# Next batch's rows turned in every attention unit, its first two Q slices in the last unit, and one PSUM bank each for V and K

## The chip, the cores and the metric

The kernel runs on one core of a Trainium2 chip. The metric is the device time of one execution in microseconds (us). TensorE (PE in the profile) multiplies and transposes, VectorE (DVE), ScalarE (ACT) and GpSimd (POOL) do the elementwise work, and SyncE (SP) issues most transfers.

## What is computed

A pre-norm transformer layer on four batches of 1024 tokens with 1024 channels: block-local attention with 16 heads, a set of 64 global query tokens per head that replace their rows of the result, and a linear layer.

```python
        q = _split_heads(hidden_states @ Wq + bq)
        k = _split_heads(hidden_states @ Wk + bk)
        v = _split_heads(hidden_states @ Wv + bv)
        ctx = _local_attention(q, k, v)      # query block of 128, keys from 64 before it to 64 behind it
        idx = _global_index(q)               # token 0, the 62 of largest norm, the last token, per head
        qg = jnp.take_along_axis(q, idx[..., None], axis=-2)
        g_scores = jnp.einsum('nhqd,nhkd->nhqk', qg, k) / math.sqrt(d)
        g_probs = jax.nn.softmax(g_scores, axis=-1)
        g_ctx = jnp.einsum('nhqk,nhkd->nhqd', g_probs, v)
        ctx = ctx.at[bn, bh, idx].set(g_ctx)
...
        w = weight * scale_weight[:, None]
        out = jnp.einsum('bsi,oi->bso', x, w) + bias
...
    x = L0_attn_hidden_states                # 4 batches, 1024 tokens, 1024 channels, 16 heads
    x = x + _L0_attn_ref(_layernorm(x, axis=-1), L0_attn_Wq, L0_attn_bq, L0_attn_Wk, L0_attn_bk, L0_attn_Wv, L0_attn_bv)
    x = x + _L0_ffn_ref(_layernorm(x, axis=-1), L0_ffn_weight, L0_ffn_scale_weight, L0_ffn_bias)
```

## The kernel before

Everything is float32 with split operands: each matmul operand x is held as x_hi (rounded) and x_lo (the rest), and a product is three matmuls, hi\*hi, lo\*hi and hi\*lo. A projection slice is 128 output channels (a pair of heads). One **half** of a slice (512 of the 1024 tokens) is 24 matmuls of 128x512 into one of the two PSUM banks of `proj`; a **part** is 12 of these 24.

For each batch n the program runs two phases.

- **The Q phase**: slices 0 to 7 of Q. PE projects a half, ACT takes it out of PSUM with the bias (`q_out`), PE turns it back to token rows (`turn_q`), ACT copies (`q_nat_out`) and SP stores it, and DVE takes the norms (`norm_of`). From slice 4 on DVE also runs the search for the largest norms of the first eight heads (`top_find`, 24 steps, then `top_rows`). PE turns norms into rows twice per batch (`turn_norms`). At the end of the phase V and K of pair 0 are projected.
- **Eight units**, one per pair of heads (`attend`, hp = 0 to 7; they are called unit 0 to unit 7 here). A unit has four steps of local attention (`scores`, `maxima`, `exps`, `turn_p`, `p_hi_out`, `p_lo_out`, `weigh`) and one global step. Between them, at eight fixed places, PE does part(0) to part(7). In units 0 to 6 these are the projections of V and K for the next unit. In unit 7 they are the transposes of the eight row tiles of the next batch (or, after the last batch, of the linear layer's weight), 8 transposes each, into the banks of `proj`; ACT then writes xT_hi and DVE xT_lo from there.

Each engine's order is written out by hand; nothing is scheduled. DVE's order at the end of a unit is `global_maxima`, `row_moments`, `pv_sums(3)`, `split_q` (two passes over 1024 columns), `k_lo_out(0)`, `gp_lo_out`, the layer norm's roots, `row_normalise`, `k_lo_out(1)`, `g_out`. In unit 3 the last steps of the second norm search and `top_rows` stand ahead of `split_q`. `k_lo_out` reads a half of K from its bank and is what frees it (`proj_free`); for V it is `v_out` on ACT.

In the code before, a half belongs to a bank: half 0 of V and of K goes to bank 0, half 1 of both to bank 1. In units 0 to 6 the parts are V half 0, V half 1, K half 0, K half 1, two parts each:

```python
b = k // 4
project_half(n, PAIRS + 2 + 2 * hp + b, b, n * BUFS + PAIRS // 2 + 1 + hp, (k // 2) % 2, (k % 2,))
```

`misc` is one more PSUM bank, in which the pieces of V (`turn_v`, three groups), the padded global query (`turn_gq`) and a small part of the global probabilities are turned, one after the other. `v_lo_out(2)` on DVE is the last reader of the third V group. POOL splits weights (`split`: a cast and a subtraction per slice, 1.1 and 2.5 us on average by the page) and scales the step results (`normalise`). SP is in order as well: rows, weights, stores.

## Time and profile before

| | |
|---|---|
| time, median of 3 runs | 2275.86 us (2275.55 to 2278.52) |
| span of the profiled execution | 2275.5 us |
| PE busy | 2192.1 us, 96% |
| weight loads, DVE, ACT, POOL busy | 82%, 68%, 37%, 26% |
| granted TensorE clock, mean | 0.991 |
| chain that ended last | PE 79%, DVE 15%, issue 4%, ACT 2% |

The chain that ended last is the way back from the last instruction to what released it. A timeline row says when a group of equal instructions began (us from the start of the span), how long it took, engine, line, what it writes and reads, how many, and in brackets how long the engine was idle before and what ended that. A window row gives the length of a stretch, each engine's busy time in it with its count, and then the granted clock.

### The profile page before, as it was taken

What the parts mean: (1) busy time and instruction counts of PE and PEld (TensorE: products, weight loads), DVE (VectorE), ACT (ScalarE), POOL (GpSimd) and SP (SyncE); (2) the same over time, 40 slices, a digit from 0 to 9 for tenths busy, and PEclk for the clock granted to TensorE, in tenths of its full rate; (3) what the DMA queues carried; (4) which work ended last, traced back from release to release, by engine and by line L of the source; (5) the groups of instructions that cost most, each with busy time, mean ns of one, the idle gap of its engine ahead of it and who ended that gap; (6) DMA issues with size and microseconds to landing.
All of it is one profiled execution on the core that took longest, in us unless ns stands there. A gap on an engine that the chain in (4) does not pass through costs nothing.

```text
span 2275.5 us, 41042 instructions
## 1 busy us (share of the span) xinstructions
PE 2192.1 (96%) x13024; PEld 1863.5 (82%) x13024; DVE 1536.0 (68%) x3466; ACT 834.3 (37%) x2202; POOL 600.8 (26%) x468
## 2 busy tenths in 40 slices
PE   5999999989999999899999998999999988999999
PEld 4878888878788888787888887878888876888887
DVE  6587776664877756638777657387776577666664
ACT  2324444443254454532544445224544550000000
POOL 2232222223332221232322321324123123222211
PEclk9999999999999999999999999999999998999999
DMA  3321111112311111122111111221111113333331
GB/s 125 88 86 43 51 57 42 51 33 80 98 42 51 58 42 51 33 82 89 49 51 51 48 51 33 79 91 51 45 48 58 44 35 139 134 124 138 138 133 70
DMA packets 106436, 159.97 MB, mean 70 GB/s; under 512 B 9648, under 2 KB 75254, under 8 KB 106352
## 3 DMA queue, kind: packets, MB, share of 16 engines
q1 hardware_dynamic: 98416, 140.03, 19.0%
q10 hardware_dynamic: 4608, 16.78, 1.8%
q0 software_dynamic: 3328, 2.17, 0.5%
q8 instruction: 38, 0.62, 0.1%
q14 instruction: 46, 0.38, 0.1%
HBM read 107.53 MB, written 51.41 MB: 70 GB/s over the span
## 4 chain that ended last, share of the span: by engine, by line
PE 79%; DVE 15%; issue 4%; ACT 2%; DVEq 0%; DMA 0%; SPq 0%; ACTq 0%
PE proj L441 36%; PE proj L684 15%; PE pv L534 8%; PE turn L524 5%; PE score L509 4%; PE pv L579 3%; PE score L560 2%; DVE x_norm L1034 2%; DVE top_idx L1032 2%; DVE top_val L1030 2%; PE misc L547 1%; PE turn L675 1%; DVE q_sq L997 1%; DVE norms L999 1%; PE turn L570 1%
## 5 line engine op out<-in xcount | busy, mean ns | idle before, releaser
L441 PE MATMUL proj<-xT_hi,w_hi 128*128 128x512 f32 x1536 | 402.5, 404 | 4.0 <-DVE xT_lo L991 2.3
L441 PE MATMUL proj<-xT_hi,w_lo 128*128 128x512 f32 x1536 | 405.7, 397 | 0.0
L441 PE MATMUL proj<-xT_lo,w_hi 128*128 128x512 f32 x1536 | 381.8, 391 | 0.0
L441 PEld LDWEIGHTS proj<-xT_lo,w_hi 128*128 128x128 f32 x1536 | 288.8, 188 | 62.3
L441 PEld LDWEIGHTS proj<-xT_hi,w_lo 128*128 128x128 f32 x1536 | 282.5, 189 | 62.6
L441 PEld LDWEIGHTS proj<-xT_hi,w_hi 128*128 128x128 f32 x1536 | 275.9, 189 | 60.2 <-issue 4.1
L781 ACT ACTIVATE probs<-score,neg_max 128x256 f32<-128x256 f32 (+1 forms) x512 | 228.7, 459 | 164.9 <-DVE neg_max L1079 99.2
L336 POOL TENSOR_TENSOR ctx_out<-pv_sum,row_inv 128x256 f32<-128x256 f32 x128 | 87.6, 684 | 706.4 <-DVE pv_sum L1116 706.4
L328 POOL TENSOR_TENSOR w_lo<-w_raw,w_hi 128x1024 fp32r<-128x1024 f32 x98 | 242.3, 2472 | 7.9
L326 POOL CAST w_hi<-w_raw 128x1024 fp32r<-128x1024 f32 x98 | 106.5, 1086 | 486.6 <-PE proj L441 284.2
L534 PE MATMUL pv<-v_nat,pT_lo 128*128 128x128 f32 x1024 | 198.3, 275 | 0.0
L534 PE MATMUL pv<-v_nat,pT_hi 128*128 128x128 f32 x1024 | 194.3, 271 | 3.1 <-DVE pT_lo L1095 2.8
L1116 DVE TENSOR_TENSOR pv_sum<-pv,pv_lo 128x256 f32<-128x256 f32 x128 | 54.2, 424 | 186.0 <-ACT pv_lo L805 186.0
L534 PEld LDWEIGHTS pv<-v_nat,pT_hi 128*128 128x128 f32 x1024 | 161.6, 191 | 15.4 <-issue 5.5
L1095 DVE TENSOR_TENSOR pT_lo<-turn,pT_hi 128x512 fp32r<-128x512 f32 x256 | 164.6, 684 | 12.0 <-ACT pT_hi L794 9.6
L997 DVE TENSOR_TENSOR q_sq<-q_nat 128x512 f32<-128x512 f32 x64 | 63.4, 991 | 148.7 <-ACT q_nat L731 147.7
L534 PEld LDWEIGHTS pv<-v_nat,pT_lo 128*128 128x128 f32 x1024 | 155.4, 192 | 0.0
L421 POOL TENSOR_TENSOR q_store<-q_store,bias_b 128x1024 f32<-128x1024 f32 x32 | 76.7, 2400 | 286.2 <-DVE q_store L1288 284.8
L794 ACT CAST pT_hi<-turn 128x512 fp32r<-128x512 f32 x256 | 138.6, 597 | 7.7 <-PE turn L524 2.1
L524 PE MATMUL turn<-ident,probs 128*128 128x128 f32 (+1 forms) x1024 | 137.9, 277 | 3.5 <-ACT probs L781 3.5
L722 ACT ACTIVATE qT_cur<-proj,bq_c 128x512 f32<-128x512 f32 x64 | 44.1, 689 | 216.3 <-PE proj L441 216.3
L524 PEld LDWEIGHTS turn<-ident,probs 128*128 128x128 f32 (+1 forms) x1024 | 113.1, 138 | 6.6 <-ACT probs L781 6.5
(147 smaller groups left out, 3598.8 us busy)
## 6 DMA issues: line engine op xcount, KB each, us to landing
w_raw<-in_wstream SPq DMA_DIRECT2D x98, 512.0 KB, 3.8
q_store<-in_rows SPq DMA_DIRECT2D x36, 512.0 KB, 3.5
x_buf<-in_rows SPq DMA_DIRECT2D x36, 512.0 KB, 3.3
q_rows<-q_nat SPq DMA_DIRECT2D x64, 256.0 KB, 2.3
ctx_rows<-ctx_out SPq DMA_DIRECT2D x128, 128.0 KB, 1.8
q_store<-ctx_rows SPq DMA_DIRECT2D x32, 512.0 KB, 4.1
out<-q_store ACTq DMA_DIRECT2D x32, 512.0 KB, 2.6
bias_b<-in_bias_ffn SPq DMA_DIRECT2D x1, 512.0 KB, 7.9
```

Of the source, the lines that this page charges most:

```text
L326: pool.tensor_copy(w_hi[b][:, :], w_raw[b][:, :]).then_inc(w_hi_set, 1)
L328: pool.tensor_tensor(w_lo[b][:, :], w_raw[b][:, :], w_hi[b][:, :].bitcast(F32), ALU.subtract).then_inc(w_split[b], 1)
L336: pool.tensor_tensor(ctx_out[:, s % 2].rearrange("p b h d -> p h b d"), pv_sum[:, s % 2].rearrange("p (h b) d -> p h b d", h=2), row_inv[: ...
L441: mm = pe.matmul(proj[:, half, :], w[b][:, k * P:k * P + P], x[:, k, half * HALF:half * HALF + HALF], start=(m == 0), stop=(m == 23), skip ...
L509: mm = pe.matmul(score[:, at:at + hi - lo], qs[r, i * BLK:i * BLK + BLK], ks[r, lo:hi], start=(first and b == 0), stop=stop, skip_group_ch ...
L524: mm = pe.transpose(turn[0:rows, col:col + P], probs[:, src:src + rows], ident[:, :])
L534: mm = pe.matmul(pv[:, g * P:g * P + P], pt[:, (g * 2 + c) * P:(g * 2 + c) * P + P], v_nat[:, 2 * s + b + c, h, :], start=(m == 0), stop=( ...
L684: mm = pe.matmul(proj[:, half, :], x[b][:, k * P:k * P + P], w[:, k, half * 512:half * 512 + 512], start=(m == 0), stop=(m == 23), skip_gr ...
L781: last = act.activation(probs[:, at:at + hi - lo], score[:, at:at + hi - lo], ACT.Exp, bias=neg_max[:, g:g + 1], accum_out=row_sum[:, g:g ...
L794: act.copy(pT_hi[:, h * 512:h * 512 + 512], turn[:, h * 512:h * 512 + 512]).then_inc(pT_hi_set, 1)
L997: dve.tensor_tensor(q_sq[:, :], src, src, ALU.mult).then_inc(q_squared[h], 1)
L1095: dve.tensor_tensor(pT_lo[:, cols], turn[:, cols], pT_hi[:, cols].bitcast(F32), ALU.subtract).then_inc(pT_set, 1)
```

## The change

The diff does four things.

1. **Rows.** In unit i the row tile i of the next batch, already normalised (now into a tile of its own, `xn_row`), is turned in two halves of four transposes through `misc` (`turn_row`): the first right behind `weigh(0)`, the second behind part(2). ACT copies each half to `q_store` (`keep_row`). ACT and DVE make xT_hi and xT_lo of whole tiles from there (`row_hi`, `row_lo`): tiles 1 to 4 in unit 6, tiles 5, 6, 0 and 7 in unit 7. Part(0) to part(7) of unit 7 no longer transpose.
2. **First two Q slices.** The parts of unit 7 now project Q slices 0 and 1 of the next batch, token half by token half, Q0 in bank 0 and Q1 in bank 1; ACT takes them out (`early_q_out`), and the Q phase begins with their transposes (`turn_early_q`) and slice 2. After the last batch these parts are empty.
3. **V and K by token half.** The parts are now V half 0, K half 0, V half 1, K half 1; V always goes to bank 0, K always to bank 1. The same holds at the end of the Q phase. There `k_lo_out(0)` moves ahead of two steps of the norm search on DVE, and ACT takes out K half 0 ahead of V half 1.
4. **Weights and start.** POOL's and SP's order follow: the next V slice is split behind `normalise(2)` and waits for V's second half; four Q slices are split ahead of the scatter. At the program's start half 0 of Q0 and Q1 is projected among the last turned rows.

The core of the diff:

```diff
+            def project_pair(first, count, b, half, part):
+
+                if part == 0:
+                    if half == 0:
+                        pe.wait_ge(w_split[b], count + 2)
+                    pe.wait_ge(proj_free[b], first + half + 1)
+                mm = project(b, half, b, part)
+                if part == 1:
+                    mm.then_inc(proj_done[b], 1)
...
+            def turn_row(n, u, i, h):
+
+                if h == 0:
+                    pe.wait_ge(xn_set, n * TILES + i + TILES + 1)
+                    pe.wait_ge(m_set, u * MISC + 3)
+                apart(pe)
+                if h == 1:
+                    pe.wait_ge(row_out, 2 * u + 1)
+                for k in range(KC // 2):
+                    c = h * HALF + k * P
+                    mm = pe.transpose(misc[:, k * P:k * P + P], xn_row[:, c:c + P], ident[:, :])
+                mm.then_inc(x_turned, 1)
...
                 def part(k):
 
-                    if not ahead:
-                        if k == 0:
-                            pe.wait_ge(proj_free[1], at_k + 2)
-                        for i in LAST_TILES[k]:
-                            t = ROW_ORDER[i]
-                            turn_rows(last_rows if i == 0 else q_store[:, t, :], (n + 1) * TILES + i, proj_banks)
-                    else:
-                        b = k // 4
-                        project_half(n, PAIRS + 2 + 2 * hp + b, b, n * BUFS + PAIRS // 2 + 1 + hp, (k // 2) % 2, (k % 2,))
+                    if not following:
+                        return
+                    if last and k % 4 == 0:
+                        pe.wait_ge(xT_set, (n + 1) * X_COUNT + (k // 4 + 1) * (X_COUNT // 2))
+                    project_pair(first + 2, n * BUFS + PAIRS // 2 + 1 + hp, (k // 2) % 2, k // 4, k % 2)
...
-                dve.scalar_tensor_tensor(kT_lo[:, tok], proj[:, h, :], bk_c[:, bass.ds(hp, 1)],
-                                         kT_hi[:, tok].bitcast(F32), ALU.add, ALU.subtract).then_inc(proj_free[h], 1)
+                dve.scalar_tensor_tensor(kT_lo[:, tok], proj[:, 1, :], bk_c[:, bass.ds(hp, 1)],
+                                         kT_hi[:, tok].bitcast(F32), ALU.add, ALU.subtract).then_inc(proj_free[1], 1)
...
+            def row_lo(n, i):
+
+                t, nth = ROW_ORDER[i], (EARLY_ROWS + LATE_ROWS + (TILES - 1,)).index(i)
+                dve.wait_ge(xT_hi_set, (n + 1) * X_COUNT + 2 * nth + 2)
+                apart(dve)
+                at = (slice(None), slice(None), slice(t * P, t * P + P))
+                dve.tensor_tensor(xT_lo[at], q_store[:, i, :].rearrange("p (k t) -> p k t", t=P), xT_hi[at].bitcast(F32),
+                                  ALU.subtract).then_inc(xT_set, 2)
...
+                k_lo_out(n, 0, 0)
                 top_find(n, 1, 0)
                 top_find(n, 1, 1)
-                k_lo_out(n, 0, 0)
```

PE at the end of units 0 to 6, from part(5) to the first global product, before (w_hi1 and w_lo1 are the weights of K, w_hi0 and w_lo0 those of V; rows with ISA or REGISTER_ALU only wait or count):

```order
L441 MATMUL proj<-xT_hi,w_lo1 128x512 x4
L441 MATMUL proj<-xT_lo,w_hi1 128x512 x8
L565 ISA
L570 MATMUL misc<-ident,probs 64x128 [waits exp_set]
L570 MATMUL turn<-ident,probs 128x128 x7
L570 MATMUL turn<-ident,probs 64x128
L441 MATMUL proj<-xT_hi,w_hi1 128x512 [waits proj_free1]
L441 MATMUL proj<-xT_hi,w_hi1 128x512 x7
L441 MATMUL proj<-xT_hi,w_lo1 128x512 x8
L441 MATMUL proj<-xT_lo,w_hi1 128x512 x8
L579 MATMUL pv<-v_nat,pT_hi 128x256 [waits pv_free,pT_set]
```

and now:

```order
L460 MATMUL proj<-xT_hi,w_lo0 128x512 x4
L460 MATMUL proj<-xT_lo,w_hi0 128x512 x8
L626 ISA
L631 MATMUL misc<-ident,probs 64x128 [waits exp_set]
L631 MATMUL turn<-ident,probs 128x128 x7
L631 MATMUL turn<-ident,probs 64x128
L460 MATMUL proj<-xT_hi,w_hi1 128x512 [waits proj_free1]
L460 MATMUL proj<-xT_hi,w_hi1 128x512 x7
L460 MATMUL proj<-xT_hi,w_lo1 128x512 x8
L460 MATMUL proj<-xT_lo,w_hi1 128x512 x8
L640 MATMUL pv<-v_nat,pT_hi 128x256 [waits pv_free,pT_set]
```

The last 12 matmuls of K half 0 have become those of V half 1. The group behind the transposes is K half 1 in both, and it waits for bank 1; that bank's last group was V half 1 before and is K half 0 now.

PE at the end of the Q phase, from `turn_norms` to unit 0, before:

```order
L480 MATMUL score<-ident,norms 8x128 [waits norm_set]
L480 MATMUL score<-ident,norms 8x128 x7
L441 MATMUL proj<-xT_hi,w_lo0 128x512 x4
L441 MATMUL proj<-xT_lo,w_hi0 128x512 x8
L441 MATMUL proj<-xT_hi,w_hi1 128x512 [waits proj_free0,w_split1]
L441 MATMUL proj<-xT_hi,w_hi1 128x512 x7
L441 MATMUL proj<-xT_hi,w_lo1 128x512 x8
L441 MATMUL proj<-xT_lo,w_hi1 128x512 x8
L441 MATMUL proj<-xT_hi,w_hi1 128x512 [waits proj_free1]
L441 MATMUL proj<-xT_hi,w_hi1 128x512 x7
L441 MATMUL proj<-xT_hi,w_lo1 128x512 x8
L441 MATMUL proj<-xT_lo,w_hi1 128x512 x8
```

and now:

```order
L524 MATMUL score<-ident,norms 8x128 [waits norm_set]
L524 MATMUL score<-ident,norms 8x128 x7
L460 MATMUL proj<-xT_hi,w_lo0 128x512 x4
L460 MATMUL proj<-xT_lo,w_hi0 128x512 x8
L460 MATMUL proj<-xT_hi,w_hi1 128x512 [waits proj_free1]
L460 MATMUL proj<-xT_hi,w_hi1 128x512 x7
L460 MATMUL proj<-xT_hi,w_lo1 128x512 x8
L460 MATMUL proj<-xT_lo,w_hi1 128x512 x8
```

K half 0 has left the place between V half 1 and K half 1 (it stands ahead of V half 1 now), and K half 1 follows V half 1 at once.

DVE in unit 7, from the second step's maxima to the last piece of V, before (line 991 there reads the turned row from PSUM in two halves):

```order
L1079 TENSOR_REDUCE neg_max<-score 128x2 [waits scored]
L1079 TENSOR_REDUCE neg_max<-score 128x2
L1105 REGISTER_ALU
L1109 RECIPROCAL row_inv<-row_sum 128x4 [waits ctx_set,exp_set]
L989 REGISTER_ALU
L991 TENSOR_TENSOR xT_lo<-proj,xT_hi 128x4x128 [waits xT_hi_set0]
L991 TENSOR_TENSOR xT_lo<-proj,xT_hi 128x4x128 [waits xT_hi_set1]
L1061 REGISTER_ALU
L1064 TENSOR_TENSOR v_nat<-misc,v_nat 128x2x64 [waits m_hi_set]
```

and now:

```order
L1192 TENSOR_REDUCE neg_max<-score 128x2 [waits scored]
L1192 TENSOR_REDUCE neg_max<-score 128x2
L1218 REGISTER_ALU
L1222 RECIPROCAL row_inv<-row_sum 128x4 [waits ctx_set,exp_set]
L1101 REGISTER_ALU
L1104 TENSOR_TENSOR xT_lo<-q_store,xT_hi 128x8x128 [waits xT_hi_set]
L1174 REGISTER_ALU
L1177 TENSOR_TENSOR v_nat<-misc,v_nat 128x2x64 [waits m_hi_set]
```

The split of a row stays ahead of the last piece of V; what is new is that PE waits for this last piece before it turns a row (`turn_row` above).

## Rows read from the trace of the kernel before

**Rows 1.** Page, section 1: busy us, share, instructions of each engine.

```profile
PE 2192.1 (96%) x13024; PEld 1863.5 (82%) x13024; DVE 1536.0 (68%) x3466; ACT 834.3 (37%) x2202; POOL 600.8 (26%) x468
```

**Rows 2.** Waits of PE: waiter, awaited; us in total, times, longest.

```profile
PE score L480 <- DVE norms L999: 8.3, 4, 2.2
...
PE misc L553 <- DVE q_pad L1122: 7.2, 4, 1.8
```

**Rows 3.** Windows over the four units 7: busy us (count) by engine, clock, DMA.

```profile
461.90:500.40 38.50, 31.60 (x253) 27.40 (x253) 28.49 (x58) 25.01 (x71) 5.78 (x6) 0.96 0.13 42
...
sum 154.00, PE 126.34 PEld 109.64 DVE 114.46 ACT 100.29 POOL 23.14; mean PE 31.58 PEld 27.41 DVE 28.61 ACT 25.07 POOL 5.78
```

**Rows 4.** Timeline of PE, end of unit 6 of the first batch.

```profile
448.20 0.63 PE L560 MATMUL score<-kT_lo,gq_hi 128*128 128x512 f32 x2
...
451.38 2.01 PE L441 MATMUL proj<-xT_lo,w_hi 128*128 128x512 f32 x8
...
454.13 2.07 PE L441 MATMUL proj<-xT_hi,w_hi 128*128 128x512 f32 x8
```

**Rows 5.** Timeline of DVE, the same stretch.

```profile
448.94 1.23 DVE L1088 TENSOR_REDUCE neg_max<-score 128x1 f32<-128x1024 f32 x1 [2.68 <-PE score L560]
...
451.85 0.42 DVE L1116 TENSOR_TENSOR pv_sum<-pv,pv_lo 128x256 f32<-128x256 f32 x1 [0.50 <-ACT pv_lo L805]
...
452.91 1.52 DVE L1009 SCALAR_TENSOR_TENSOR qT_lo<-q_store,qT_hi 128x1024 fp32r<-128x1024 f32 x1
454.43 0.75 DVE L1015 SCALAR_TENSOR_TENSOR kT_lo<-proj,bk_c,kT_hi 128x512 fp32r<-128x512 f32 x1
```

**Rows 6.** Timeline at part(6): first and last of 24 units, then unit 3.

```profile
198.21 0.94 PE L441 MATMUL proj<-xT_hi,w_hi 128*128 128x512 f32 x3
198.43 0.74 DVE L1015 SCALAR_TENSOR_TENSOR kT_lo<-proj,bk_c,kT_hi 128x512 fp32r<-128x512 f32 x1
...
1833.02 0.94 PE L441 MATMUL proj<-xT_hi,w_hi 128*128 128x512 f32 x3
...
1833.31 0.75 DVE L1015 SCALAR_TENSOR_TENSOR kT_lo<-proj,bk_c,kT_hi 128x512 fp32r<-128x512 f32 x1
...
325.67 2.07 PE L441 MATMUL proj<-xT_hi,w_hi 128*128 128x512 f32 x8
...
329.02 0.75 DVE L1015 SCALAR_TENSOR_TENSOR kT_lo<-proj,bk_c,kT_hi 128x512 fp32r<-128x512 f32 x1
...
338.61 0.63 PE L547 MATMUL misc<-ident,vT 128*128 128x128 f32 x4 [0.88 <-DVE v_nat L1064]
```

**Rows 7.** Timeline, end of the second batch's Q phase: PE, then ACT.

```profile
607.08 1.03 PE L480 MATMUL score<-ident,norms 128*8 128x128 f32 x8 [2.07 <-DVE norms L999]
...
616.65 2.11 PE L441 MATMUL proj<-xT_hi,w_hi 128*128 128x512 f32 x8 [0.34 <-ACT vT L755]
...
615.02 1.00 ACT L738 COPY x_norm<-score 8x1024 f32<-8x1024 f32 x1 [11.56 <-DVE idx_skip L1052]
...
616.50 0.66 ACT L761 ACTIVATE kT_hi<-proj,bk_c 128x512 fp32r<-128x512 f32 x1
```

**Rows 8.** Timeline of PE and DVE in unit 7 of the first batch.

```profile
466.86 0.50 PE L509 MATMUL score<-kT_hi,qT_hi 64*128 64x256 f32 x4
...
472.55 1.29 DVE L991 TENSOR_TENSOR xT_lo<-proj,xT_hi 128x512 fp32r<-128x512 f32 x2 [1.79 <-ACT xT_hi L715]
473.75 0.28 DVE L1064 TENSOR_TENSOR v_nat<-misc,v_nat 128x128 fp32r<-128x128 f32 x1
```

**Rows 9.** Timeline of PE at the start, and windows with the granted clock.

```profile
44.96 3.36 PE L441 MATMUL proj<-xT_hi,w_hi 128*128 128x512 f32 x8 [2.25 <-DVE xT_lo L991]
...
484.70:492.00 7.30, 7.25 (x45) 6.81 (x46) 5.52 (x10) 3.65 (x8) 0.61 (x1) 0.77 0.07 20
604.00:612.00 8.00, 5.93 (x31) 4.59 (x30) 7.27 (x12) 0.00 (x0) 0.00 (x0) 1.00 0.49 165
...
1885.00:1890.00 5.00, 1.97 (x8) 1.57 (x8) 1.72 (x7) 1.01 (x1) 3.78 (x5) 0.50 0.32 124
```

513 lines of the change are left out of this document (290 added, 223 removed).

## The prediction

> **What bounds the kernel now.** I read the page first: PE is busy 96% of the span [rows 1]. So the time is PE's work plus PE's idle time, and the change moves PE's work without adding or removing a matmul. What is left to ask is where PE idles before and where it will idle after. I went along PE's timeline for every idle piece over 0.12 us; they sum to some 79 us. Nearly half is the first 30 us and the entry into the linear layer, which stay. What the change can touch is this. The four units 7 last 38.5 us each, and PE is busy in 31.6 of it: 6.9 us idle [rows 3], of which 1.8 us is the padded query [rows 2]. In the same units the clock falls: 0.77 on average over 7.3 us, which is 1.2 GHz for almost half of it, so 7.3 x 0.23 = 1.7 us of work is lost [rows 9]. Each Q phase ends with a wait of PE for the norms, 8.3 us in four times [rows 2, 7], and one of 0.3 us for ACT [rows 7]. At the start PE idles 2.25 us before Q0's second half, and the eight matmuls behind it take 3.36 us instead of 2.07 [rows 4, 9]. Units 0 to 6 have no idle time at all, but for 0.88 us early in unit 4 [rows 6]. There PE has no slack to give: whatever the change makes it wait for comes on top.
>
> **Term 1, the new bank order, 24 units: +24 us.** Before, part(6) (K half 1) writes bank 1, which V half 1 left early in the unit. Now bank 1 holds K half 0 until DVE's `k_lo_out(0)` has read it. In unit 6 part(6) starts at 454.13. On DVE the chain to `k_lo_out(0)` starts when the global scores are there: maxima at 448.94, `row_moments`, `pv_sums` at 451.85, `split_q` to 454.43, `k_lo_out(0)` 454.43 to 455.18 [rows 4, 5]. Nothing in the change shortens this order, and PE's work between the global scores and part(6) is the same in size. So PE waits 455.18 - 454.13 = 1.05 us. In the first of the 24 units (0, 1, 2, 4, 5, 6 of four batches) the same difference is 0.96 us, in the last 1.04 us [rows 6]. To this comes the way from DVE to PE, some 0.1 us. It may be less: `qT_lo` takes 1.52 us [rows 5] where POOL scales a result beside it, and 1.23 us in unit 3, where POOL rests; POOL's scaling now moves behind the weight split, whose cast can overlap the end of `qT_lo` instead. Bounds 0.7 and 1.15 us, I take 1.0, near the measured difference: 24 x 1.0 = 24. Nothing hides it: PE is in order, and part(6), part(7), the global product and the next unit stand behind it. K half 0 itself being ready earlier helps nothing, since `split_q` stands ahead of its reader.
>
> **Term 2, unit 3 of each batch: +13.6 us.** Here the end of the norm search and `top_rows` stand ahead of `split_q`. `k_lo_out(0)` runs from 329.02 to 329.77, part(6) started at 325.67: 4.1 us, with the way to PE 4.2; POOL's split beside `split_q` can add up to 0.6. I take 4.3. DVE is caught up then, so the 0.88 us in unit 4 goes [rows 6]. 4 x (4.3 - 0.9) = 13.6, bounds 12.8 and 16.
>
> **Term 3, the end of the Q phase: +3.8 us.** Before, PE starts the last projected half at 616.65, 0.1 us after ACT's `v_out`, which follows the norm copy at 615.02 to 616.02. Now K half 0 takes the norm wait's place, so that wait goes, and PE has done V half 1 by about 613.9 (two halves of 5.5 us, `turn_norms` and V half 1 from 596.1 + 5.9). But K half 1 needs bank 1, that is the norm copy, then `k_hi_out(0)` (start 615.9, 0.66 us as in the row at 616.50), then `k_lo_out(0)` on DVE (0.75 us): 617.5 or 617.6 [rows 5, 7]. That is 0.95 us later than before. The chain that ends at the norm copy is DVE's search, and it doesn't change. So the 2.1 us of the norm wait is not won: 4 x 0.95 = 3.8. Bounds 0 and 5.
>
> **Term 4, three units 7 with work in them: -15.3 us.** The idle time of 6.9 us and the clock's 1.7 us go, 8.6 each. The parts are long enough to hide the step chain, as in units 0 to 6, except at two places. First, `turn_row` waits for the last piece of V. Before, in unit 7, `scores(1)` starts at 466.86 and this piece is done at 474.03, 7.2 us later, since a row's split (472.55) stands ahead of it [rows 8]. Now one more ACT copy of 0.7 us (`early_q_out`) stands there too, and DVE enters the unit some 0.9 us late, after two extra row splits in unit 6 (1.3 us each by [rows 8], half of it hidden in that unit's new wait). So the piece comes 8.8 us after `scores(1)`; PE gets there after 0.9 (scores) + 2.8 (part) + 0.1 + 1.8 (`weigh`) = 5.6 us. Wait: 3.2 us. Second, part(4) needs the last row split, which ends 0.2 to 0.5 us late. 3 x (8.6 - 3.2 - 0.3) = 15.3. In units 0 to 6 the piece comes 0.25 us before `weigh(0)` ends, so there the new wait costs nothing. The extra splits in unit 6 fall into DVE's idle 2.68 us [rows 5]; the copies on ACT, a third busy, cost nothing; the transposes are as many as before. At the ends: all waits vanish (-25.8), or they double (-5).
>
> **Term 5, the last batch's unit 7: +1 us.** It has no projections. Its first half is bound by the chain over ACT and DVE, which keeps its row splits and gains two copies of 0.6 us; the 1.9 us or so that PE spent on transposes late in the unit partly come off. Bounds -3 and +4.
>
> **Term 6, the start: -3.5 us.** Half 0 of Q1 stands where PE waited: -2.25, and the slow matmuls, -1.3. Bounds -4 and 0.
>
> Moved at no cost: Q0's and Q1's transposes (same count, under slice 2's half), SP's loads (they land in under 4 us and have a unit's time), POOL's splits (V's third in the unit starts at part(5)'s end and is needed 10 us later, for 3.5 us of work; K's first is needed one part pair earlier, 3 us to spare behind the gather in unit 0).
>
> **Sum**, from the profiled 2275.5 us: 24 + 13.6 + 3.8 - 15.3 + 1 - 3.5 = +23.6, so 2299 us. The median of the runs is 2275.9, next to it.
>
> **A rule beside the rows.** V's two halves now share bank 0 as K's share bank 1. For V the rows show no cost: ACT takes half 0 out right behind the second step's exponentials, and part(4) comes some 12 us later; only K's reader is late [rows 4, 5]. The Trainium skill, "Perfetto Trace Analysis", section Matmuls, asks for independent matmul groups to rotate through different PSUM banks so that one is emptied beside the next, and so speaks against both pairs. By it V's pair would cost its copy too, by the copy's 0.7 us in 28 units some 19 us more, 2318 us; by the rows it costs nothing.
>
> **Rivals.**
> (a) Faster, 2258 us. It is decided at part(6): if `k_lo_out(0)` ends before PE gets there, terms 1 and 2 vanish. Then the sum is 3.8 - 15.3 + 1 - 3.5 and -3.5 for unit 4's idle time: -17.5. For it: ACT finishes K half 0 earlier, and POOL is away from `qT_lo`. Against it: that is worth 0.3 us, and 1.05 are needed [rows 5, 6]. 9 in 100; with the last unit's waits gone too it would be 2248.
> (b) Slower still by the clock, 2318 us. The rows: behind idle times of 2.1 us in dense work the clock stays at 1.00; behind 7.4 us it stands at 0.50 [rows 9]. The new idle times of 4.3 (4 of them), 3.7 (4, terms 2 and 3) and 3.2 us (3) lie between. If each lets it fall, at 1.7 us each as in [rows 9], that is 11 x 1.7 = 19 on top. 18 in 100. The Trainium skill, "TensorE: Matmul & The Clock Gate", section HAM oscillation, has idle gaps between bursts of matmuls throttle the clock again; by that rule this is the case, and [rows 9] bear it out only for the longest gap.
> (c) The change doesn't bring what it moves, 2314 us: in unit 7 the new projections wait for their rows as long as PE idled before (part(0) on the tiles split in unit 6, part(4) on row 7), and term 4 is nil. For it: DVE and ACT have row work in every step. Against: 5.1 us of margin per unit. 8 in 100.
> (d) The waits are real but short, terms 1 to 3 near their low bounds and few in unit 7: 2275.5 + 17 + 12.8 - 24 + 1 - 3.5 = 2279, up to 2290. 12 in 100, a third of it within 0.2% of before.
>
> **Numbers.** Forecast 2299 us (2290 to 2308), 53 in 100. A measurement of this kernel tells a difference of 0.2%, 4.6 us, from none. Faster by more: (a), 9. Within: from (d), 4. Slower: 87. The range from 2280 to 2320 leaves out (a) and the lowest of (d), some 13 in 100, and little above.
>
> **What would show it.** In the page after, PE idle before the projection line with DVE's `kT_lo` as releaser, some 24 + 17 us over 28 times, and 15 us more at the end of the Q phases. Units 0 to 6 lasting 42.5 + 0.9 (row transposes) + 1.0. Three waits of 3 us before a row transpose in unit 7 for `v_nat`, none for `q_pad` in three of four batches. If PE shows no wait at part(6), term 1 and the forecast are wrong; if windows behind the waits have a clock under 0.9, it is (b).

## The result, and the profile after

The changed kernel takes 2352.6 us (median of four runs, 2351.9 to 2353.3) where the kernel before takes 2276.4 us (2275.6 to 2278.5). The ratio is 1.0335, 95% interval 1.0323 to 1.0347. The direction was forecast, the size was not: 2299 us, in a range of 2280 to 2320.

The page of the changed kernel, its span and section 1, beside [rows 1]:

```profile
span 2350.3 us, 40763 instructions
...
PE 2218.1 (94%) x13024; PEld 1879.8 (80%) x13024; DVE 1553.2 (66%) x3434; ACT 857.4 (36%) x2218; POOL 597.6 (25%) x464
```

PE has as many matmuls as before, 26 us more busy time (its matmuls ran slower) and 49 us more idle time. What PE waited for, beside [rows 2] (waiter, awaited; us in total, times, longest):

```profile
PE proj L460 <- DVE kT_lo L1128: 51.8, 32, 6.8
...
PE misc L608 <- DVE v_nat L1177: 13.8, 8, 3.1
PE misc L508 <- DVE v_nat L1177: 8.1, 7, 1.7
...
PE turn L537 <- issue: 7.2, 2, 4.0
```

The waits for the norms (8.3 us) and for `q_pad` (7.2 us) are gone, as said. The wait for `kT_lo` is there, as said, and larger than the other new ones together. The last row was not forecast at all.

To see where the time went I cut both traces at the first scores of each unit and at the end of each unit 7, and took each piece's length, the idle pieces of PE in it and its mean granted clock. "Clock loss" is length x (1 - clock), from the clock records of the trace (the two digits that a window prints give it within 0.3 us for a unit and 0.8 us for the first Q phase); part of it lies in idle time, so the columns overlap.

| part | before us | after us | more | of it idle / clock loss | forecast |
|---|---|---|---|---|---|
| start and first Q phase | 163.5 | 162.1 | -1.5 | -0.2 / +3.4 | -2.6 |
| 24 units (0, 1, 2, 4, 5, 6) | 1023.6 | 1065.8 | +42.2 | +12.8 / 0 | +41.9 |
| four units 3 | 170.1 | 211.1 | +41.0 | +27.3 / +13.7 | +20.7 |
| three units 7 and the Q phases behind them | 483.5 | 471.6 | -11.9 | +2.4 / +12.0 | -31.2 |
| last unit 7 | 38.5 | 42.8 | +4.3 | +6.2 / +8.5 | +1 |
| linear layer | 396.3 | 397.1 | +0.9 | +0.5 / 0 | 0 |
| sum | 2275.5 | 2350.3 | +75 | +49 / +37 | +29.8 |

The forecast column is the prediction's six terms with the row transposes put where they now stand: 0.89 us a unit (a unit without any wait takes 43.37 us in the experiments, 42.48 before), so 21.4 us in the 24 units, 3.6 in units 3, and 18.7 us out of the three units 7. It sums to 29.8 and not to 23.6, and the difference is an error of mine: the 6.2 us of transposes that units 0 to 6 of the last batch now hold were not on PE's path before. They stood in the last unit, which waits for a chain over ACT and DVE anyway.

**Units 3.** DVE and POOL and PE around part(6) of the first batch's unit 3, beside the last rows of [rows 6] (start us, us, engine, line; in brackets the idle time before it and its releaser):

```profile
330.28 1.04 POOL L330 CAST w_hi<-w_raw 128x1024 fp32r<-128x1024 f32 x1 [8.10 <-PE proj L460]
330.43 1.03 DVE L1156 TENSOR_SCALAR idx_eq<-idx_f 8x62 f32<-8x62 f32 x2
...
331.38 2.40 DVE L1157 TENSOR_SCALAR idx_row<-idx_f,row_base 8x64 f32<-8x64 f32 x1
331.39 2.34 POOL L332 TENSOR_TENSOR w_lo<-w_raw,w_hi 128x1024 fp32r<-128x1024 f32 x1
...
337.10 0.74 DVE L1128 SCALAR_TENSOR_TENSOR kT_lo<-proj,bk_c,kT_hi 128x512 fp32r<-128x512 f32 x1
...
337.90 3.78 PE L460 MATMUL proj<-xT_hi,w_hi 128*128 128x512 f32 x8 [6.81 <-DVE kT_lo L1128]
...
341.48 2.38 PE L460 MATMUL proj<-xT_hi,w_lo 128*128 128x512 f32 x8
```

An operation on 8x64 elements takes 2.40 us, about as long as POOL's subtraction beside it (2.34); at the end of the Q phase, with POOL at rest, the same line takes 0.23. And behind the wait eight matmuls take 3.78 us instead of 2.07.

**The end of the Q phase** (second batch), beside [rows 7]: ACT's norm copy, K half 0 out, DVE's reader, PE:

```profile
630.28 1.00 ACT L821 COPY x_norm<-score 8x1024 f32<-8x1024 f32 x1 [11.23 <-DVE idx_skip L1165]
631.19 0.67 ACT L844 ACTIVATE kT_hi<-proj,bk_c 128x512 fp32r<-128x512 f32 x1
...
631.89 0.75 DVE L1128 SCALAR_TENSOR_TENSOR kT_lo<-proj,bk_c,kT_hi 128x512 fp32r<-128x512 f32 x1 [1.54 <-ACT kT_hi L844]
...
632.70 3.54 PE L460 MATMUL proj<-xT_hi,w_hi 128*128 128x512 f32 x8 [3.04 <-DVE kT_lo L1128]
```

From the norm copy to PE it is 2.42 us, 1.63 before: 0.8 later, where 0.95 was forecast. What the forecast lacks is again the slow eight.

**The start of the Q phase**, which had no idle time of this size before:

```profile
531.59 1.24 PE L640 MATMUL pv<-v_nat,pT_lo 128*128 128x256 f32 x9
536.80 1.92 PE L537 MATMUL turn<-ident,q_store 128*128 128x128 f32 x8 [3.97 <-issue]
538.37 2.96 PE L460 MATMUL proj<-xT_hi,w_hi 128*128 128x512 f32 x8
```

Nothing releases it: ACT's last copy for it ended at 531.5. The trace has a record of PE's sequencer there, the branch back to the head of the batch loop, from 530.63 to 536.43. Before, the same branch is recorded from 501.89 to 505.77, and PE worked on, on 24 projection matmuls that were already queued, and idled only 0.36 us behind them. The change puts only the 18 matmuls of the global product (2.3 us) and nothing else ahead of it.

**Unit 7**, beside [rows 8]: DVE's small operations of the row's root at the end of unit 6, POOL's split, DVE's first maxima and PE (first batch):

```profile
479.13 0.98 DVE L1047 TENSOR_TENSOR ln_sq<-ln_rstd 128x1 f32<-128x1 f32 x1
...
480.18 2.37 POOL L332 TENSOR_TENSOR w_lo<-w_raw,w_hi 128x1024 fp32r<-128x1024 f32 x1
480.34 2.23 DVE L1049 SCALAR_TENSOR_TENSOR ln_rstd<-ln_less,ln_rstd 128x1 f32<-128x1 f32 x1
...
486.23 1.28 DVE L1195 TENSOR_REDUCE neg_max<-score 128x1 f32<-128x192 f32 x4
...
488.31 0.63 PE L608 MATMUL misc<-ident,vT 128*128 128x128 f32 x4 [3.09 <-DVE v_nat L1177]
...
498.75 0.63 PE L508 MATMUL misc<-ident,q_store 128*128 128x128 f32 x4 [1.69 <-DVE v_nat L1177]
```

### The profile page after: what moved, and what is told of

Same layout as the page of the kernel before. It is cut to its first block, busy times and chain, and to the rows that moved or that the text cites. A ratio compares the mean times of both kernels' runs of the same rounds, so it can differ in the third digit from the quotient of the medians.

```text
span 2350.3 us, 40763 instructions
## 1 busy us (share of the span) xinstructions
PE 2218.1 (94%) x13024; PEld 1879.8 (80%) x13024; DVE 1553.2 (66%) x3434; ACT 857.4 (36%) x2218; POOL 597.6 (25%) x464
## 4 chain that ended last, share of the span: by engine, by line
PE 72%; DVE 18%; issue 7%; ACT 2%; DVEq 1%; DMA 0%; ACTq 0%; SPq 0%; another core or an unknown queue 0%
PE proj L460 32%; PE proj L742 15%; PE pv L596 7%; PE turn L586 5%; PE score L571 4%; PE pv L640 2%; PE score L621 2%; DVE x_norm L1147 2%; DVE top_idx L1145 2%; DVE top_val L1143 2%; DVE neg_max L1201 2%; PE misc L608 1%; PE misc L508 1%; PE turn L733 1%; DVE kT_lo L1128 1%
## 5 line engine op out<-in xcount | busy, mean ns | idle before, releaser
L460 PE MATMUL proj<-xT_hi,w_hi 128*128 128x512 f32 x1536 | 418.8, 416 | 51.8 <-DVE kT_lo L1128 51.8
L460 PE MATMUL proj<-xT_hi,w_lo 128*128 128x512 f32 x1536 | 413.2, 400 | 0.0
L460 PEld LDWEIGHTS proj<-xT_hi,w_hi 128*128 128x128 f32 x1536 | 285.7, 196 | 119.5 <-DVE kT_lo L1128 60.9
L354 POOL TENSOR_TENSOR ctx_out<-pv_sum,row_inv 128x256 f32<-128x256 f32 x128 | 82.0, 641 | 755.1 <-DVE pv_sum L1229 749.1
L330 POOL CAST w_hi<-w_raw 128x1024 fp32r<-128x1024 f32 x96 | 111.9, 1166 | 544.4 <-PE proj L460 421.9
L332 POOL TENSOR_TENSOR w_lo<-w_raw,w_hi 128x1024 fp32r<-128x1024 f32 x96 | 237.5, 2474 | 7.8
L844 ACT ACTIVATE kT_hi<-proj,bk_c 128x512 fp32r<-128x512 f32 x64 | 44.3, 693 | 205.7 <-PE proj L460 205.7
L1110 DVE TENSOR_TENSOR q_sq<-q_nat 128x512 f32<-128x512 f32 x64 | 57.1, 892 | 90.5 <-ACT q_nat L814 84.1
```

Source lines behind the costliest of these rows:

```text
L330: pool.tensor_copy(w_hi[b][:, :], w_raw[b][:, :]).then_inc(w_hi_set, 1)
L332: pool.tensor_tensor(w_lo[b][:, :], w_raw[b][:, :], w_hi[b][:, :].bitcast(F32), ALU.subtract).then_inc(w_split[b], 1)
L354: pool.tensor_tensor(ctx_out[:, s % 2].rearrange("p b h d -> p h b d"), pv_sum[:, s % 2].rearrange("p (h b) d -> p h b d", h=2), row_inv[: ...
L460: mm = pe.matmul(proj[:, bank, :], w[b][:, k * P:k * P + P], x[:, k, half * HALF:half * HALF + HALF], start=(m == 0), stop=(m == 23), skip ...
```

## The experiments

Four readings had to be told apart: DVE's order ahead of `k_lo_out(0)`; POOL's split in DVE's way; the clock behind a wait; and PE's branch. Each experiment is the changed kernel with one edit, e8 to e11 with several. One caution for all of them: in the changed kernel PE waits 3.0 us in the four units 0 ahead of a row transpose (the L508 row above, with the 1.7 us of the units 7), in e2 and e5, which touch nothing there, it doesn't, and the clock's loss in the first Q phase moves between 1.7 and 8.5 us from kernel to kernel. In e4 the pieces that the edit doesn't touch are 11 us shorter together. So 5 to 11 us of a difference can be of this sort, and the readings below go by the pieces of one profiled execution each.

**e1_klo_first.** DVE's order alone.

```diff
                 pv_sums(u, 3)
+                if not last:
+                    k_lo_out(n, hp + 1, 0)
                 top_norms(5)
                 if not last:
                     split_q(u + 1, hp + 1)
-                    k_lo_out(n, hp + 1, 0)
```

> The changed kernel with one order changed on DVE: in each unit k_lo_out(0), the reader that frees bank 1, stands ahead of the norm search's last steps, top_rows and split_q instead of behind them. Theory (the wait at part(6) is DVE's order alone: ACT has K half 0 out 1.7 us before DVE gets to it, 426.44 against 428.18 in unit 5 of the first batch): the waits of 0.49 us in 24 units and of 6.81 us in the four units 3 go, and with the latter the low clock behind them (3.2 to 3.7 us a unit): 24 x 0.5 + 4 x 10.2 = 53 us less than 2352.6, so 2300 us, PE's wait for kT_lo at the projection line down from 51.8 us to the 13 us of the Q phases. Rival A (the search steps only push their lateness on, to gp_lo_out, or to the next unit's maxima): units 3 keep a wait of some 4 us elsewhere, 2320 us. Rival B (the bank order costs for another reason than this wait): 2340 or more.

Measured: 2329.0 us, 24 less, half of what the theory said. All waits at part(6) are gone and units 0 to 2 take 43.4 to 43.9 us. But others have come (waits of PE, then DVE and POOL at the end of unit 4 of the first batch):

```profile
PE misc L608 <- DVE v_nat L1177: 28.7, 13, 4.4
...
PE pv L640 <- DVE pT_lo L1214: 14.9, 7, 2.7
PE proj L460 <- DVE kT_lo L1128: 12.8, 4, 3.3
```

```profile
380.69 2.96 DVE L1059 TENSOR_SCALAR q_store<-q_store,ln_mv,ln_rstd 128x1024 f32 x1 [0.29 <-DVE ln_rstd L1056]
380.72 2.39 POOL L332 TENSOR_TENSOR w_lo<-w_raw,w_hi 128x1024 fp32r<-128x1024 f32 x1
```

`row_normalise` takes 0.81 us in unit 3 and 2.96 here, where POOL's subtraction starts in the same moment; DVE enters unit 5 late, and PE waits there 1.7 us for the first V piece, and 1.4 us in unit 6. With PE earlier, POOL's split falls on other operations of DVE. In unit 3 the search and `top_rows` (now with 2.49 us for `idx_eq`) make `gp_lo_out` late instead: 2.7 us ahead of the global product. Rival A was right in kind on unit 3 (2.7 us, not 4), and the theory on part(6): the wait was DVE's order, and half of its worth was lateness that goes on to the next reader.

**e2_written_out.** PE's loop over the batches written out; the short loops inside a batch stay.

```diff
...
-            with pe.Fori(0, BATCH - 1) as n:
-                batch(n, True)
-            batch(BATCH - 1, False)
+            for n in range(BATCH):
+                batch(n, n < BATCH - 1)
```

> The changed kernel with PE's loop over the batches written out, so that PE has no backward branch between two batches; nothing else differs. Theory: the idle time of 3.97 and 3.22 us ahead of turn_early_q at the start of the second and third Q phase (no releaser in the profile, and none at the start of the fourth, which is written out already) is PE's branch, which was hidden behind 24 queued projection matmuls in the kernel before (branch record 501.89 to 505.77 there). Both waits go and the slow matmuls behind them (2.96 us for eight instead of 2.07, and on): 7.2 + 3 = 10 us less, 2342 us. Rival (the Q phase waits there for ACT's early_q_out, for POOL or for SP): the two gaps stay, 2352 us.

Measured: 2335.1 us (2327.8 to 2337.3), 17 less. The start of the second Q phase now:

```profile
529.04 1.24 PE L641 MATMUL pv<-v_nat,pT_lo 128*128 128x256 f32 x9
530.12 1.03 PE L538 MATMUL turn<-ident,q_store 128*128 128x128 f32 x8
530.91 2.08 PE L460 MATMUL proj<-xT_hi,w_hi 128*128 128x512 f32 x8
```

The second Q phase is 7.1 us shorter and the third 5.0. Up to the wait for `kT_lo` at their ends it is 5.6 and 5.0: 10.6 us for two branches, 7.2 of idle time and 3.4 of clock. The other 1.5 us come behind that wait, where the clock stays up in one of the two phases, as it does in the fourth (2.6 us), which has no branch in either kernel; this and the units 0 are of the sort named above. (The profiled execution is the fastest of the four, 2327.8 us; the others take 2333.8 to 2337.3.) The branch is shown.

**e3_norm_copy_later.** The end of the Q phase in another order (ACT; on DVE `k_lo_out(n, 0, 0)` ahead of `split_q` and `top_rows`; PE waits for `norm_rows_set` ahead of unit 0).

```diff
                 v_out(n, 0, 0)
-                norms_out(n, 1)
                 k_hi_out(n, 0, 0)
                 v_out(n, 0, 1)
+                norms_out(n, 1)
                 k_hi_out(n, 0, 1)
...
```

> The changed kernel with the end of the Q phase put in another order: ACT takes K half 0 and V half 1 out ahead of the second norm copy, DVE's k_lo_out(0) stands ahead of split_q and top_rows, and PE waits for the norm copy before the first scores instead. Theory: the wait of 3.04 to 3.26 us before K half 1 goes, and with it the eight slow matmuls behind it (3.54 us instead of 2.07): 4 x (3.1 + 1.5) = 18 us less, 2334 us. Rival (the search on DVE is the chain: PE then waits as long before the first scores of unit 0, or for a later maxima): half of it comes back, 2343 us or more.

Measured: 2336.1 us, 16.5 less. The wait before K half 1 is gone in all four phases, which are 21 us shorter together in the profile; in unit 0 another came, 2.9 us long in the first batch and 0.9 to 1.3 in the rest, for POOL, which splits V's next weights behind the index rows that wait for `top_rows`:

```profile
PE proj L460 <- POOL w_lo L332: 6.2, 4, 2.9
```

**e4_filled_wait.** 28 transposes of the identity in that same wait.

```diff
+                for _ in range(28):
+                    pe.transpose(misc[:, 0:P], ident[:, :], ident[:, :])
                 for part in range(2):
                     project_pair(n * SLICES + PAIRS, n * BUFS + PAIRS // 2, 1, 1, part)
```

> The changed kernel with 28 transposes of the identity (0.11 us each, 3.1 us in all) put into PE's wait before K half 1 at the end of each Q phase; they compute nothing that is used. Theory (the slow matmuls behind the wait, 3.54 us for eight instead of 2.07, and the windows with a clock under 1.00 come from PE standing idle for 3 us): with the wait filled, K half 1 starts as late as before but runs at full clock: 4 x 1.5 to 4 x 3 = 6 to 12 us less, 2343 us (0.996 to 0.998). Rival (the slow matmuls come from the data or from what runs beside them, not from the idle time): no gain, the same 3.5 us, 2352.6 us, or some 1 us more.

Measured: 2337.1 us, 15.5 less, and under half of it belongs to the edit. PE does 3.2 us of useless work where it stood still, starts K half 1 no earlier, and is done sooner:

```profile
626.55 3.22 PE L707 MATMUL misc<-ident 128*128 128x128 f32 x28
629.92 2.11 PE L460 MATMUL proj<-xT_hi,w_hi 128*128 128x512 f32 x8 [0.15 <-DVE kT_lo L1130]
```

From the start of K half 1 to unit 0 it is 5.7 us in all four phases, where it was 7.1, 7.1, 7.2 and 8.3: 7.0 us less, which is what the clock cost behind this wait. In the fourth phase, where this is PE's only wait, the clock's loss falls from 3.4 us to nothing. In the second and third the clock stays low longer behind PE's branch instead (a loss of 3.4 us in the whole phase as before), and they are no shorter. The other pieces, which the edit doesn't touch, are 11 us shorter, 4.7 of it in the units 7, where waits of the same length cost less clock.

**e12_unit3_wait_filled.** The same in unit 3: 60 transposes ahead of part(6), unit 3 taken out of PE's loop for it.

```diff
                 turn_gp(u)
+                for _ in range(fill):
+                    pe.transpose(score[:, 0:P], ident[:, :], ident[:, :])
                 part(6)
...
```

> The changed kernel with 60 transposes of the identity (0.11 us each, 6.6 us) put into PE's wait of 6.81 us ahead of part(6) in unit 3; nothing uses them, and every wait and every order stays. It prices the clock's share of that unit's 10.2 us. Theory (6.81 us are the wait, the rest is the clock, which falls because PE stands idle): unit 3 takes 44.1 + 6.8 = 50.9 us or less instead of 52.5 to 53.1, eight matmuls behind the wait take 2.07 us instead of 3.78, the clock's loss of 3.2 to 3.7 us a unit goes: 4 x 1.5 to 4 x 3.5 = 6 to 14 us less, 2343 us. Rival (the slow matmuls come with K half 1 itself or with what runs beside it): no change, 2352 us.

Measured: 2341.4 us, 11 less, 8.5 of it in the four units 3. They take 50.66 us each instead of 52.5 to 53.1, at clock 1.00:

```profile
339.32 2.11 PE L460 MATMUL proj<-xT_hi,w_hi 128*128 128x512 f32 x8 [0.29 <-DVE kT_lo L1133]
```

So of a unit 3's 10.3 us more, 0.9 are the row, 6.8 are idle, 1.9 to 2.4 the clock (8.5 us in the four), and some 0.5 us stands around the wait itself, as around the short one of the 24 units (0.3 us there).

**e5_unit3_split_held.** POOL's split of V's weights in unit 3 waits for `k_lo_out(0)`.

```diff
                 pool.wait_ge(raw_in[b], 16 * count + 16)
+                if hold is not None:
+                    pool.wait_ge(proj_free[1], hold)
...
```

> The changed kernel, with POOL's split of V's next weights in unit 3 alone held back until DVE's k_lo_out(0) is done; the order on DVE and PE is untouched. Theory: 2.7 us of the 6.81 us that PE waits in unit 3 are top_rows' small operations stretched beside POOL's two 128x1024 operations (1.03 and 2.40 us where the same lines take 0.28 and 0.23 us in the Q phase), so the wait falls to 4.1 to 4.3 us, as forecast, and the split, 3.5 us in an interval of 12, delays nobody: 4 x 2.6 = 10 us less, 2342 us; 2336 us if the clock behind the shorter wait stays up in some units. Rival (the operations are long for another reason, their waits on one another, or the wait is ACT's): 6.8 us as before, 2352 us.

Measured: 2338.3 us, 14 less, 10.8 of it in the four units 3. DVE's line is short again, and the wait is close to what the prediction's own working gives for it without POOL (4.1 to 4.3 us):

```profile
327.66 0.23 DVE L1161 TENSOR_SCALAR idx_row<-idx_f,row_base 8x64 f32<-8x64 f32 x1
...
332.02 3.78 PE L464 MATMUL proj<-xT_hi,w_hi 128*128 128x512 f32 x8 [3.91 <-DVE kT_lo L1132]
```

That the first eight are as slow behind 3.91 us as behind 6.81 says that the longer wait cost no more clock. The difference of the two waits, 2.9 us, is what the two lines of `top_rows` lost beside POOL: 0.75 us (1.03 against 0.28) and 2.16 us (2.40 against 0.23).

**e6_key_split_later.** POOL's split of K's weights waits for the unit's first maxima.

```diff
                 i = PAIRS + 3 + 2 * hp
+                pool.wait_ge(max_set, 2 * ((n * PAIRS + hp) * EVENTS) + 2)
                 split(n, i, 1,
...
```

> The changed kernel with POOL's split of K's weights (in unit 7 that of Q slice 1) started after the first step's maxima of the unit instead of at its start, so that it lies beside DVE's PSUM readers and not beside row_roots and row_normalise. Theory: at the start of the three units 7 PE's wait of 3.09 us for v_nat comes from 3.1 us by which DVE is late (0.98 and 2.23 us for operations of 0.16 us), so it goes; the 1.69 us before turn_row stays or halves, and the 0.5 to 1.0 us waits in units 0 and 4 go: 3 x 3.1 + 3 x 1.5 of clock + 4 = 16 us less, 2336 us. Rival (the three extra row splits make DVE late, not POOL): the 3.09 us stay within 1 us, 2348 us.

Measured: 2342.1 us, 10.5 less, but mostly not where it was expected. The 3.09 us are gone from the three units 7, and this stands there instead, ahead of the row transpose:

```profile
493.86 1.09 PE L509 MATMUL misc<-ident,q_store 128*128 128x128 f32 x4 [4.27 <-DVE v_nat L1178]
```

So POOL made DVE late at the unit's entry, as the theory says. Further on DVE idles 2.9 us for ACT's half (`row_hi`) of a row split that stands ahead of the V piece in its queue, which is the rival's sort of cause; and POOL's moved split now stretches another row split (2.44 us instead of 1.22). The units became 0.6 to 1.5 us shorter, no more; the rest of the gain is in units 0 and 4.

**e7_search_spread.** Six search steps in units 0 to 2, three in unit 3.

```diff
-                attend(n, 0, 0, top=range(3, 8))
-                attend(n, 1, 0, top=range(8, 13))
-                attend(n, 2, 0, top=range(13, 18))
-                attend(n, 3, 0, top=range(18, TOP_STEPS))
+                attend(n, 0, 0, top=range(3, 9))
+                attend(n, 1, 0, top=range(9, 15))
+                attend(n, 2, 0, top=range(15, 21))
+                attend(n, 3, 0, top=range(21, TOP_STEPS))
```

> The changed kernel with the norm search spread otherwise: six steps of it in each of the units 0, 1 and 2 instead of five, and three in unit 3, so that top_rows ends in the middle of unit 3 and not ahead of k_lo_out(0). Theory (term 2 is the search and top_rows standing in DVE's queue at one place): unit 3's wait falls from 6.81 us to 0.5 us and the low clock behind it goes, 4 x (6.3 + 3.3) = 38 us less; the sixth step makes k_lo_out(0) late by 1.3 us in the units 0 to 2, 12 x 1.3 = 16 us more; so 2330 us, waits of 1.7 to 1.8 us in units 0 to 2 with the clock at 1.00. Rival A (a wait of 1.8 us also lets the clock fall): 12 x 3 = 36 us more on top, 2366 us. Rival B (unit 3 keeps a wait of over 2 us): 2340 us or more.

Measured: 2363.8 us, 11 more than the changed kernel. Rival A said 2366, but with waits of 1.8 us; the waits came out longer, so that its number is right in part by luck. Unit 3 is at 44.13 us, the same as its neighbours: term 2 is shown to be the search and `top_rows`. But units 0 and 1 wait 2.5 us and unit 2 waits 4.77, and behind 2.51 us the clock falls in seven units of eight. Windows of 6 us behind the wait in unit 0 of the first and of the second batch (length, busy time of PE, PEld, DVE, ACT, POOL, granted clock, DMA share, GB/s):

```profile
198.30:204.30 6.00, 5.98 (x19) 4.88 (x20) 4.73 (x21) 0.00 (x0) 2.10 (x2) 0.72 0.24 70
680.60:686.60 6.00, 5.99 (x28) 5.05 (x29) 4.71 (x21) 0.14 (x1) 2.21 (x3) 1.00 0.27 76
```

**e8_all_repairs.** The edits of e1, e2, e3, e6 and e7 together, and in unit 7 each row split behind the V piece that it stood ahead of.

> The changed kernel with all repairs together: k_lo_out(0) first, PE's batches written out, the norm copy behind K half 0, K's split behind the first maxima, the search spread to six steps a unit, and in unit 7 each row split behind the V piece it stood ahead of. Theory (the move itself is sound and its cost is these waits): no wait at part(6), none over 0.5 us in units 0 to 6, at most 1 us in unit 7, no branch: 2353 - 53 - 17 - 17 - 3 x 6 = 2248 us, with the clock up in the Q phases, 1.2% under the kernel before. Rival A (DVE is full: what is taken from one wait comes up at the next, as the 2.70 us ahead of the global product in unit 3 and the 1.4 to 1.7 us in units 5 and 6 did when only k_lo_out was moved): 2280 us. Rival B: PE's branch and code cost as much elsewhere, 2290 us.

Measured: 2280.0 us, 73 less than the changed kernel, 1.0011 (1.0002 to 1.0021) of the kernel before. The Q phases 2 to 4 take 96.4 us without idle time. What waits still:

```profile
PE misc L610 <- DVE v_nat L1180: 23.2, 17, 2.9
...
PE proj L461 <- POOL w_lo L332: 8.0, 7, 2.8
```

The first are 1.06 to 1.25 us behind each unit with a sixth search step, and 2.2 us in unit 7; the second come of POOL's later splits in units 0 and 4. Rival A's time was right, and its reason in part.

**e9_repairs_placed.** As e8, with the search in its old places, in unit 3 POOL's split behind `split_q`, and in unit 0 the weight splits ahead of the index columns and gather.

```diff
+                split_even(n, PAIRS + 2)
                 store_rows(n, 0)
-                split_even(n, PAIRS + 2)
+                split_key(n, 0, False)
                 load_columns(n, 0)
                 gather(n, 0)
...
```

> As e8_all_repairs, with three things put otherwise, each for a wait that its trace shows: the search again in five steps a unit and six in unit 3 (the sixth step gave 1.06 to 1.25 us of wait before the next unit's second V turn in twelve places); in unit 3 POOL's split of V's weights behind split_q (so that top_rows isn't stretched); in unit 0 the splits of V's and K's weights ahead of the index columns and the gather, and those of units 0 and 4 not held for the maxima (PE waited 0.3 to 2.8 us for POOL's w_lo there). Theory (each wait has its own place and price): 2280 - 12 x 1.1 - 4 x 1.7 - 2 of clock = 2258 us, unit 3 at 44 us, the units 1, 2, 5 and 6 at 43.4 us without idle time. Rival (DVE's lateness moves to another place, unit 3 and 4 above all, as with k_lo_out alone): 2270 us or more.

Measured: 2280.3 us: no gain. Units 1, 2, 5 take 43.37 us and unit 3 43.6, as expected, but units 0 and 4 take 46 to 48:

```profile
PE misc L616 <- DVE v_nat L1186: 31.1, 12, 2.9
```

These are 2.6 and 2.9 us at the second V turn. `top_rows` and the search steps ahead of a unit make DVE enter it late, also with POOL's splits elsewhere. The rival was right (e11 takes these waits away by moving the search).

**e10_last_unit_filled.** e9 with ten transposes of the identity in each place of the last unit where a projection would stand.

```diff
                     if not following:
+                        for m in range(10):
+                            pe.transpose(proj[:, 0, 0:P], ident[:, :], ident[:, :])
                         return
```

> As e9_repairs_placed, with ten transposes of the identity (0.11 us each) in each of the eight places of the last unit of all where no projection stands any more; nothing uses them. In e8 this unit takes 44.0 us, 8.5 us of them idle, and the clock there costs 16.7 us. Theory (the low clock comes from PE's sparse work): with 8.8 us of filler the clock stays up longer and the unit takes 39 us, 5 us less than e9. Rival (the unit is bound by the chain over ACT and DVE, the clock costs only PE time that would be idle): no gain, or up to 4 us more where the filler stands in PE's way.

Measured: 2279.0 us, which the timing can't tell from e9. In the profiled execution the unit itself went from 41.1 to 38.8 us, and its clock up (the windows of that unit in e9, then in e10):

```profile
1841.60:1882.70 41.10, 31.97 (x196) 28.23 (x195) 23.41 (x48) 22.07 (x61) 2.46 (x4) 0.73 0.17 54
```

```profile
1842.00:1880.80 38.80, 32.99 (x276) 29.95 (x275) 23.41 (x48) 21.88 (x61) 2.46 (x4) 0.96 0.12 36
```

The unit is bound by its chain for the most part; the clock was worth some 2 us of it. (Without filler it takes 41.2 to 44.6 us in all these kernels, with it 38.9 here and 38.0 in e11.)

**e11_search_and_splits_moved.** e10 with DVE's work put where it idles.

```diff
                 top_find(n, 1, 1)
-                top_find(n, 1, 2)
                 k_lo_out(n, 0, 1)
...
                 top_norms(4)
+                top_norms(5)
...
-                rows_lo(1)
                 rows_lo(2)
+                rows_lo(3)
                 global_maxima(u)
```

(`rows_lo(1)` goes ahead of `pv_sums(u, 2)`, `rows_lo(4)` ahead of `gp_lo_out`, ACT's copies with them; the search stands in steps 2 to 7, 8 to 13, 14 to 19 and 20 to 23. Two of e9's settings of POOL are put back as well: its split of V's weights in unit 3 no longer waits for `split_q`, and that of K's in unit 4 waits for the first maxima again.)

> As e10_last_unit_filled, with DVE's work moved to where it idles, for the three places that still wait there: units 0 and 4 (2.6 and 2.9 us before the second V turn, DVE late by the search steps ahead of the unit) and unit 7 (2.2 us, DVE late by two row splits at the end of unit 6). The search has two steps instead of three ahead of unit 0, and six in each unit, the sixth beside the fifth ahead of the global maxima, where DVE waited 1.5 to 2.7 us for PE, so that top_rows ends before unit 3's fourth step; three of the four row splits of unit 6 stand ahead of the global maxima. Theory: 4 x 4 + 4 x 4 + 3 x 3.5 = 42 us less than 2279: 2238 us. Rival (the sixth step and the third row split make the global maxima late, and so part(6) or the global product): 2265 us.

Measured: 2249.1 us (2247.5 to 2249.9), a ratio of 0.9877 (0.9861 to 0.9894) to the kernel before, 104 us less than the changed kernel. The page and PE's waits of this kind:

```profile
PE 2186.6 (97%) x13104; PEld 1867.7 (83%) x13104; DVE 1538.6 (68%) x3434; ACT 857.0 (38%) x2218; POOL 603.1 (27%) x464
```

```profile
PE misc L616 <- DVE v_nat L1188: 7.2, 8, 1.1
...
PE pv L648 <- DVE pT_lo L1225: 2.3, 4, 0.6
PE proj L467 <- POOL w_lo L334: 1.5, 3, 0.7
```

Units 1, 2, 3 and 5 take 43.37 us in every batch. To the 2238 expected 11 us are missing: units 0, 4 and 6 stay up to 1.0 us longer than the others (unit 4 waits up to 0.7 us for POOL's `w_lo`), and the units 7 take 48.1 to 48.3 us, no less than in e9 (47.8), with 1.1 and 1.7 us of wait. So this kernel holds every move of the change and is faster than the kernel before: nearly all that the change cost was in what stood around the moves. Two things limit that. The 6.2 us of transposes that have come onto PE's path in the last batch are still there. And some of the repairs, the written-out loop and the filler in the last unit among them, could be made in the kernel before as well; no run does that, and none puts the old bank order into the changed kernel. So what the moves alone are worth is not measured.

## Why the prediction went wrong

The change cost 75 us in the profile and the sum gave 24. The steps that failed are these, with what each missed: term 2 had the wait in units 3 too short and no price for the clock behind it (20 us); term 4 had nothing for PE's branch between two batches (10.6 us) and took back a clock loss that stayed; the waits at the end of the Q phase had no price for the clock (7.0 us by e4); and the row transposes of the last batch were moved "at no cost" (6.2 us). The mechanism of terms 1 to 3, `k_lo_out(0)` freeing K's bank late, was right.

**Term 1 (24 x 1.0 us) was right in kind and high**: the wait is 0.49 us in the trace, under its lower bound of 0.7, and a unit with it 0.78 us longer than one without (44.15 against 43.37), 19 us. `qT_lo` took 1.23 us, as the lower bound had it, since POOL's scaling had moved. Units 0 and 4 add a few us (in unit 4 0.3 to 0.7 us of the old wait stays in three batches of four, which term 2 had counted as gone), above all a wait of 0.4 to 1.0 us ahead of the row transpose in unit 0, where the prediction had the third V piece in time; so the 24 units came out as forecast, with a part of it by chance.

**Term 2 (4 x 4.3 us) was too small by 20 us**, in two halves. The wait is 6.8 us, since 2.9 us of POOL's split fell on `top_rows`. The prediction had POOL's split of V's weights moved "at no cost", with 10 us until its own reader for 3.5 us of work, and asked what it would do to `split_q` (0.6 us), and not to the ten small operations ahead of it. Held back (e5), the wait is 3.91 us, inside what the working gives. The other half is the clock (e12). The rows of before already had such a pair, `qT_lo` at 1.52 us where POOL scales a result and 1.23 where it rests [rows 5], and I read it as a matter of 0.3 us. The Trainium skill, "SBUF — State Buffer", section Who interferes with whom, has DVE and GpSimd share one pair of ports, for the operations that it lists an exclusive lock, so that the loser stands still for the whole of the other's instruction and doesn't merely slow down. By that rule an operation of 0.23 us costs up to POOL's 2.4 us on top; the trace agrees, 2.40 us beside 2.34, and 2.96 for 0.81 + 2.15 in e1. I had the page and did not weigh it.

**Term 3 (4 x 0.95 us) was right in its chain** (0.8 us), and lacked the clock: eight matmuls in 3.54 us, and 1.4 to 2.6 us a phase by e4. Rival (b) named this place.

**Term 4 (-15.3 us) fell.** The idle time of 6.9 us did go, but in its place came 4.8 us (forecast 3.5), a clock no better than before (loss of 3.4 us a unit after, 1.7 to 3.4 before), and behind it 10.6 us for PE's branch (e2). The step that failed is an omission: the prediction has no term for the seam between two batches. It lists Q0's and Q1's transposes, which now stand first behind the branch, among what is moved at no cost; I checked each queue that work was moved past but not the sequencer's own branch, although the change takes from it the 24 matmuls that hid it. The place of the first wait was also wrong: the second V turn, and not only `turn_row`, since DVE came 3 us late and not 0.9, by POOL's split on the root's small operations.

**Term 5 (+1 us)** was +4.3, and +10.5 with the 6.2 us of transposes that the prediction moved "at no cost" out of a unit that had idle time for them. **Term 6 (-3.5 us)**: the first Q phase is 1.5 us shorter in all, with term 3's wait and 3.4 us of clock in it.

**The rivals.** (a) needed 1.05 us at part(6) and got 0.56 (1.05 less the 0.49 that PE waits). (b) was right in kind: waits of 3 to 7 us let the clock fall in most places; its price of 1.7 us a place was about right for units 3 (2.1 by e12). It gave 2318, and with the branch (11), POOL on `top_rows` (12) and the last unit (3, and 6 for the transposes) that makes 2350; what is left is within the noise of the pieces. I gave it 18 in 100 and made the forecast without any clock loss, though [rows 9] left open what lies between 2.1 and 7.4 us. (c) and (d) were wrong: no projection of unit 7 waits for its rows, and the waits are not short. The rule beside the rows priced V's pair of halves in one bank at 19 us; no projection of the changed kernel waits for ACT's `vT`, so it cost nothing. The order of DVE's steps, not the bank order, decides: e11 has the same bank order, and no wait for `kT_lo` in its attention part.

## What to carry to other kernels

When a change moves work of one engine, ask of every operation that comes to lie beside it whether the two get in each other's way, the tiny ones in a serial chain above all: they lose as much as the large ones. Look for what hides a loop's branch: it costs next to nothing only while enough queued work stands ahead of it. And price a new wait in dense work with the clock it can cost, from nothing to 2.6 us more than its length here, before anything is moved; then put the reader that frees a shared buffer first in its queue, and the long helper work where that engine idles anyway.
